# State-space stage: off products scaled on ScalarE in eight pieces, first states copied by ScalarE

## The reference

```
Y_diag = einsum('bcln,bcsn,bhcls,bcshp->bclhp', C, B, Lmat, x)
decay_states = exp(A_cs[..., -1:] - A_cs)
states = einsum('bcln,bhcl,bclhp->bchpn', B, decay_states, x)
...
new_states = einsum('bhzc,bchpn->bzhpn', decay_chunk, states)
...
Y_off = einsum('bcln,bchpn,bhcl->bclhp', C, states, exp(A_cs))
Y = (Y_diag + Y_off)
```

## Time and profile before

| | us |
|---|---|
| median of 3 runs | 2145.34 |
| lowest, highest | 2144.09, 2149.49 |
| profiled execution | 2126.43 |
| its span | 2124.7 |
| TensorE busy | 1811.0 |
| VectorE busy | 1494.5 |
| ScalarE busy | 1003.0 |
| GpSimd busy | 447.5 |

### The profile page before, as it was taken

The page is one execution under the profiler, slowest core; times in us unless marked ns, Lnnn a source line. Parts: engine busy times, 40 slices in busy tenths (PEclk is TensorE's granted clock), DMA queues, the critical chain, the costliest instruction groups (busy, mean ns, idle before and its releaser), DMA issues. The chain is left out here.

```text
span 2124.7 us, 33254 instructions
## 1 busy us (share of the span) xinstructions
PE 1811.0 (85%) x10026; PEld 1240.0 (58%) x10026; DVE 1494.5 (70%) x3126; ACT 1003.0 (47%) x2291; POOL 447.5 (21%) x411
## 2 busy tenths in 40 slices
PE   5288898898898969999945695899999898989897
PEld 2146656666666559999942253464656465646564
DVE  5668878788788761222236696878887879888885
ACT  2032242241331412212202254878797979787886
POOL 2113413314314232522111202020111102020101
PEclk9589999899898989999977797999999999999998
DMA  4501221221122119755445294143443424343311
GB/s 161 181 32 60 88 70 59 77 81 59 59 70 88 50 68 320 257 187 179 139 131 175 75 300 135 51 101 69 100 89 86 95 68 102 81 90 80 80 31 31
DMA packets 143788, 226.09 MB, mean 106 GB/s; under 512 B 17725, under 2 KB 110015, under 8 KB 143648
## 3 DMA queue, kind: packets, MB, share of 16 engines
q1 hardware_dynamic: 124464, 179.95, 27.6%
q0 software_dynamic: 19184, 44.45, 8.3%
HBM read 174.26 MB, written 50.99 MB: 106 GB/s over the span
## 5 line engine op out<-in xcount | busy, mean ns | idle before, releaser
L2239 DVE TENSOR_SCALAR att_scores<-att_psS 128x512 f32<-128x512 f32 x512 | 348.7, 681 | 74.7 <-PE att_psS L2073 60.0
L2188 ACT ACTIVATE att_prob<-att_scores,att_shift 128x512 f32<-128x512 f32 x512 | 383.3, 749 | 30.3 <-DVE att_shift L2255 30.3
L2197 ACT COPY att_pT<-att_psT 128x512 f32<-128x512 f32 x512 | 305.7, 598 | 140.3 <-PE att_psT L2081 139.9
L2081 PEld LDWEIGHTS att_psT<-ident,att_prob 128*128 128x128 f32 x2048 | 244.7, 142 | 176.9 <-issue 78.4
L2247 DVE CUSTOM_DVE_ANT_0 att_scores<-att_scores,first_decay 128x512 f32<-128x512 f32 x512 | 347.6, 679 | 0.0
L2081 PE MATMUL att_psT<-ident,att_prob 128*128 128x128 f32 x2048 | 317.0, 278 | 26.6 <-ACT att_pT L2197 26.0
L2073 PE MATMUL att_psS<-first_ks,first_qs 128*128 128x512 bf16 x512 | 197.5, 387 | 33.5 <-DVE att_scores L2239 29.4
L2095 PE MATMUL att_psO<-att_pT,att_v 128*32 128x512 f32 x1024 | 139.6, 620 | 24.5 <-ACT att_pT L2197 24.5
L1233 DVE TENSOR_TENSOR_SCAN mamba_L<-mamba_am,mamba_begin 128x1024 f32<-128x1024 f32 x64 | 145.5, 2295 | 15.0 <-PE mamba_psY L954 14.7
L1460 PEld LDWEIGHTS ffn_psH<-ffn_xT,ffn_w 128*128 128x128 f32 x1248 | 147.3, 194 | 3.6 <-issue 1.7
L1460 PE MATMUL ffn_psH<-ffn_xT,ffn_w 128*128 128x128 f32 x1248 | 147.7, 277 | 1.1 <-ACT ffn_xT L1494 1.1
(11 more groups left out here) (282 smaller groups left out, 2916.7 us busy)
## 6 DMA issues: line engine op xcount, KB each, us to landing
ffn_w<-in_w SPq DMA_DIRECT2D x39, 1024.0 KB, 5.1
mamba_am<-a_rows SPq DMA_DIRECT2D x64, 512.0 KB, 3.7
first_qs<-q_parts SPq DMA_DIRECT2D x256, 64.0 KB
first_ks<-k_parts SPq DMA_DIRECT2D x256, 64.0 KB
xn<-xn_all SPq DMA_DIRECT2D x16, 512.0 KB, 5.8
ffn_w<-in_w POOLq DMA_DIRECT2D x8, 1024.0 KB, 6.2
att_w<-in_inter POOLq DMA_DIRECT2D x7, 1024.0 KB, 6.1
att_w<-in_outer POOLq DMA_DIRECT2D x7, 1024.0 KB, 7.2
```

The costliest lines, as they stand in the source:

```text
L2081: mm = nc.tensor.transpose(ps[:, k * P:(k + 1) * P], prob[:, n % NP, k * P:(k + 1) * P], C.ident[:])
L2188: nc.scalar.activation(prob[:, n % NP], scores[:, n % NCL], ACT.Exp, bias=shift[:, h % 2, t:t + 1], accum_out=total[:, octet % 2, t, j, i: ...
L2197: nc.scalar.copy(pT[:, h % HEADS_T, :, t * P:(t + 1) * P], bank_of("turn", n)[:].rearrange("p (k q) -> p k q", k=CPB)).then_inc(pT_ready, 1)
L2239: vec.tensor_scalar(scores[:, n % NCL], psS[n % NS][:], -CLAMP, CLAMP, ALU.max, ALU.min).then_inc(clipped, 1)
```

## The change

In the state-space stage alone:

- The two first states of a batch are copied out of `psO[0]` and `psO[1]` by ScalarE, behind its copies of x, and not by VectorE. A new semaphore `state_begun` counts them; `state_ready` counts the four others. VectorE's `grow(0)` is gone, so `decays(1)` stands right behind `decays(0)`.
- `off` is on ScalarE. One instruction takes one scale for a partition, so each off product takes eight ACTIVATEs of 128x64, one for each head, with the scale from `fac`.
- ScalarE's order becomes: off(0, 1), off(1, 0), off(1, 1), squares(0), turned_tile(0), off(2, 0), off(2, 1), squares(1), turned_tile(1), off(3, 0), squares(2), turned_tile(2).

```diff
--- before.py
+++ after.py
@@ -753,6 +753,7 @@
         near_ready = s.sem("near_ready")
         xdd_ready = s.sem("xdd_ready")
         grown = s.sem("grown")
+        state_begun = s.sem("state_begun")
         state_ready = s.sem("state_ready")
         am_in = [s.sem(f"am_in{k}") for k in range(NA)]
         begun = s.sem("begun")
@@ -922,9 +923,12 @@
                             n = 2 * k + d
                             t = k if d == 0 else CPB - 1 - k
                             pe.wait_ge(xdd_ready, i * 6 + n + 1)
-                            if n >= 2:
-
-                                pe.wait_ge(state_ready, i * 6 + n - 1)
+                            if n >= 4:
+
+                                pe.wait_ge(state_ready, i * 4 + n - 3)
+                            elif n >= 2:
+
+                                pe.wait_ge(state_begun, i * 2 + n - 1)
                             else:
 
                                 pe.wait_ge(z_ready, (i + 1) * CPB)
@@ -955,7 +959,7 @@
                                                   start=False, stop=(d == 1), skip_group_check=True)
                         mm.then_inc(diag_used, 1)
                         if (d == 0 and t > 0) or (d == 1 and t < CPB - 1):
-                            pe.wait_ge(state_ready, (i + 1) * 6)
+                            pe.wait_ge(state_ready, (i + 1) * 4)
 
                             done = [2 * (t - 1) if t > 1 else 0, 2 * t][d]
                             pe.wait_ge(off_scaled, i * 6 + done)
@@ -1092,9 +1096,35 @@
                         act.wait_ge(xdt_ready, i * U)
                         act.wait_ge(xfd_ready, i * CPB)
                         nc.scalar.copy(xl[:, t], psA[(XT_AT + t) % 2][:]).then_inc(tok_ready, 1)
-                    for t in range(CPB - 1):
-                        squares(i, t)
-                        turned_tile(i, t)
+                    for d in range(2):
+                        act.wait_ge(grown, i * 6 + d + 1)
+                        if d == 0:
+
+                            act.wait_ge(off_ready, i * 6)
+                        nc.scalar.copy(state[:, d, 1 if d == 0 else CPB - 2], psO[d][:]).then_inc(state_begun, 1)
+
+                    def off(t, d, count):
+
+                        act.wait_ge(off_ready, i * 6 + count + 1)
+
+                        act.wait_ge(summed, i * CPB + t)
+                        for h in range(NH):
+                            ins = nc.scalar.activation(yo[:, d, h * HD:(h + 1) * HD], psO[d][:, h * HD:(h + 1) * HD], ACT.Copy,
+                                                       scale=fac[:, 0, d, t, h:h + 1])
+                        ins.then_inc(off_scaled, 1)
+
+                    off(0, 1, 0)
+                    off(1, 0, 1)
+                    off(1, 1, 2)
+                    squares(i, 0)
+                    turned_tile(i, 0)
+                    off(2, 0, 3)
+                    off(2, 1, 4)
+                    squares(i, 1)
+                    turned_tile(i, 1)
+                    off(3, 0, 5)
+                    squares(i, 2)
+                    turned_tile(i, 2)
                     if ahead:
                         first_tap(i + 1, 0)
                     squares(i, CPB - 1)
@@ -1255,33 +1285,19 @@
                             n = 2 * k + d
                             t = k if d == 0 else CPB - 1 - k
                             to = t + 1 if d == 0 else t - 1
-                            if n == 0:
-
-                                dve.wait_ge(off_ready, i * 6)
-                            if k:
-                                dve.wait_ge(state_ready, i * 6 + n - 1)
-                                c.step(v.tensor_tensor(by_head(scaled[:, d]), by_head(state[:, d, t]), heads(fac[:, 2, d, t]), ALU.mult))
+                            if k == 1:
+                                dve.wait_ge(state_begun, i * 2 + d + 1)
+                            else:
+                                dve.wait_ge(state_ready, i * 4 + d + 1)
+                            c.step(v.tensor_tensor(by_head(scaled[:, d]), by_head(state[:, d, t]), heads(fac[:, 2, d, t]), ALU.mult))
                             dve.wait_ge(grown, i * 6 + n + 1)
-                            if k:
-                                v.tensor_tensor(state[:, d, to], scaled[:, d], psO[d][:], ALU.add).then_inc(state_ready, 1)
-                            else:
-                                v.tensor_copy(state[:, d, to], psO[d][:]).then_inc(state_ready, 1)
+                            v.tensor_tensor(state[:, d, to], scaled[:, d], psO[d][:], ALU.add).then_inc(state_ready, 1)
 
                     def decays(u):
                         t, d = u // 2, u % 2
                         dve.wait_ge(g_ready, i * CPB + t + 1)
                         dve.wait_ge(decayed, i * U + u + 1)
                         v.tensor_tensor(L[:, u % NL], L[:, u % NL], gT[t % 2][:, d].unsqueeze(1).to_broadcast([P, NH, P]), ALU.mult).then_inc(L_ready, 1)
-
-                    def off(u, count):
-                        t, d = u // 2, u % 2
-                        if (d == 0 and t > 0) or (d == 1 and t < CPB - 1):
-                            dve.wait_ge(off_ready, i * 6 + count + 1)
-
-                            dve.wait_ge(summed, i * CPB + t)
-                            v.tensor_tensor(by_head(yo[:, d]), by_head(psO[d][:]), heads(fac[:, 0, d, t]), ALU.mult).then_inc(off_scaled, 1)
-                            return count + 1
-                        return count
 
                     def finish(t):
                         b = t % 2
@@ -1313,15 +1329,12 @@
                                                in1=x[:, t], op0=ALU.mult, op1=ALU.add).then_inc(o_ready, 1)
 
                     decays(0)
-                    grow(0)
                     decays(1)
                     grow(1)
                     grow(2)
-                    count = 0
                     for u in range(1, U + 1):
                         if 1 < u < U:
                             decays(u)
-                        count = off(u - 1, count)
                         if u >= 2 and u % 2 == 0:
                             finish(u // 2 - 1)
                         if u + NL - 1 < U:
```

## The result

The changed kernel is slower: 2173.25 us, median of 4 runs (2172.76 to 2175.7), against 2144.72 for before; the ratio is 1.0146, 95% interval 1.0127 to 1.0165, or 28.5 us. The forecast was 2182, 8.75 us too high, and the direction held. A second measurement of the same program gave 1.0130 (1.0101 to 1.0160).

The account below looks back on a forecast made before the run. VectorE was taken to set the pace by 0.60 us per tile pair, TensorE right behind; 26 us for TensorE's longer chain (3.25 us a batch) plus 11 us for lower clock, 37 us on the 2145.34 median, gave 2182 us, range 2160 to 2210.

Follow-up runs that it names:

- one_scale: The changed kernel with each off product scaled by one ACTIVATE of 128x512, head 0's factor, instead of eight of 128x64; 2134.01 us, ratio to before 0.9938.
- split_offs: The changed kernel with off products (1, 1) and (2, 1) scaled by VectorE again, the four others still on ScalarE; ratio to before 0.9899.
- turn_early_after: The changed kernel with turn_tile(0), (1) ahead of diagonal(3), (5) on TensorE, and their squares and turned_tile ahead of off(1, 1), off(2, 1) on ScalarE; 2096.62 us, ratio 0.9854.

## What to carry to other kernels

When work moves to an idle engine, look at what stands behind it in that engine's order and who waits for that: here work moved to an engine that idled for 22.36 us at a stretch (ScalarE in batch 2 of before) cost 28 us, because two of six products stood in front of a copy that TensorE needed, and moving the copy ahead of them turned +1.4% into -1.5%. A wait that makes TensorE the last should be priced twice, once for itself and once for the work behind it, which may run at half the clock; products that nobody reads are a cheap test of the second price. Judge the halves of a change apart: the copies alone gained 0.7%, the off products alone lost 1.9%.

## What the runs showed of the hardware

In batch 3 of after a wait of 2.86 us left the granted clock at 1.00 while it lasted and was followed by 3.5 us at 0.51. Over the stage fifteen of sixteen outputs behind such waits (2.4 to 2.86 us) were lengthened and one was not; behind 1.4 to 1.8 us in the same place, in one_scale, none was. In split_offs two outputs behind 0.77 us took 3.75 us, and in turn_early_after one took 3.03 us with no wait in front, so the wait just ahead doesn't decide alone. In before the clock also fell while TensorE was busy: from 311.6 to 315.6 us, behind 3.74 us of products of 128x8, its rows are busy all 4.00 us and the granted clock is 0.59. With 22 rows of matmul in the wait of after the clock stayed up, and a kernel with more work was 24.5 us shorter in its stage.

The same mean clock can cost different amounts: the stage was granted 0.93 in before and in after.

Eight ACTIVATEs of 128x64 out of PSUM, with a scale from a pointer, take 1.75 us together and 330 ns each (mean of the group), so they follow each other by 0.20 us.

The expert stage, which no edit touched, took 274 us in some executions and 292 in others, of before as of after: 292 in the four profiles known to be of chip 0, 274 in the eight of chips 4 and 5. What makes the 18.5 us was not looked into; a comparison of single executions on different chips can be wrong by it.
